# Recurrent attention with a feed-forward gate on eight cores: the key-value product moved ahead of the numerators, the output's last steps on GpSimd, and other places for the weight staging

## What is computed

```python
xn = layernorm(x)                                  # x: (8, 2048, 1024)
# recurrent (linear) attention, 16 heads of 64
q, k, v = (proj(xn, W) for W in (Wq, Wk, Wv))
qf, kf = softplus(q) + 1e-6, softplus(k) + 1e-6
kv = kv + outer(kf_t, v_t);  z = z + kf_t          # over t
out_t = (qf_t @ kv) / (qf_t . z + 1e-6)
s = out @ Wo.T
# feed-forward of the same xn, weights stored as integers with scales
h = layernorm(xn) * ln_gamma + ln_beta
y = silu(h @ dequant(fc1_q, fc1_scales) + fc1_bias)       # 4096 wide
zf = y @ dequant(fc2_q, fc2_scales) + fc2_bias
g = silu(xn + 0.5 * zf)
return x + s * g
```

## Time and profile before

| | us |
|---|---|
| median of the two runs | 4193.93 |
| the two runs | 4014.75 and 4373.1 |
| profiled execution, slowest core | 4024.7 |
| its span, first to last instruction | 4023.1 |
| TensorE matmul busy | 2843.4 (71% of the span) |
| VectorE busy | 1074.5 (27%) |
| ScalarE busy | 412.3 (10%) |
| GpSimd busy | 52.2 (1%) |

### The profile page before, as it was taken

The page is one execution under the profiler, slowest core; times in us unless marked ns, Lnnn a source line. Parts: engine busy times, 40 slices in busy tenths (PEclk is TensorE's granted clock), DMA queues, the critical chain, the costliest instruction groups (busy, mean ns, idle before and its releaser), DMA issues.

```text
span 4023.1 us, 40962 instructions; the slowest of 8 cores (4001.3 to 4023.1 us)
## 1 busy us (share of the span) xinstructions
PE 2843.4 (71%) x17088; PEld 2004.2 (50%) x17088; DVE 1074.5 (27%) x1533; ACT 412.3 (10%) x785; POOL 52.2 (1%) x103
## 2 busy tenths in 40 slices
PE   4678888757788777873087777777705668866668
PEld 3556665545566555652055555555403445544445
DVE  6332222131111211214612222222163221222221
ACT  0212222100000000000011111111100111111111
POOL 0000000000000000000100000000010000000000
PEclk9988888855665566565598888888857889888889
DMA  5111111122201122024600000000162110011110
GB/s 164 42 43 43 53 45 51 59 57 42 42 18 30 37 42 42 6 42 151 198 1 22 22 22 22 22 22 22 53 233 91 42 43 24 19 42 42 43 42 11
DMA packets 91414, 205.72 MB, mean 51 GB/s; under 512 B 37344, under 2 KB 53984, under 8 KB 85088
## 3 DMA queue, kind: packets, MB, share of 16 engines
q1 hardware_dynamic: 72368, 117.63, 9.8%
q0 software_dynamic: 14256, 68.69, 5.2%
q10 hardware_dynamic: 4608, 16.78, 1.4%
HBM read 152.75 MB, written 50.33 MB: 50 GB/s over the span
## 4 chain that ended last, share of the span: by engine, by line
PE 66%; DVE 15%; DMA 12%; issue 3%; DVEq 2%; ACT 1%; SPq 1%; POOL 0%; ACTq 0%; POOLq 0%
PE PS L142 17%; PE PS L143 17%; PE PS L144 17%; DVE AR L165 9%; DMA AR<-s 4%; PE PS L856 3%; PE PS L824 3%; DMA AR<-x_in 3%; DMA WA<-v_sc 2%; PE PS L847 2%; PE PS L850 2%; DVEq L166 2%; DVE WA L165 2%; DVE stats L165 1%; PE PS L829 1%
## 5 line engine op out<-in xcount | busy, mean ns | idle before, releaser
L142 PE MATMUL PS<-AR,WA 128*128 128x256 bf16 x3072 | 859.8, 280 | 44.0 <-DVE AR L567 29.2
L143 PE MATMUL PS<-AR,WA 128*128 128x256 bf16 x3072 | 859.6, 280 | 0.0
L144 PE MATMUL PS<-AR,WA 128*128 128x256 bf16 x3072 | 858.6, 279 | 0.0
L142 PE MATMUL PS<-WA,AR 128*128 128x512 bf16 x1536 | 597.6, 389 | 36.3 <-DVE AR L511 35.9
L143 PE MATMUL PS<-WA,AR 128*128 128x512 bf16 x1536 | 597.1, 389 | 0.0
L144 PE MATMUL PS<-WA,AR 128*128 128x512 bf16 x1536 | 595.5, 388 | 0.0
L912 PE MATMUL PS<-ident_s,AR 128*128 128x128 f32 x256 | 65.8, 426 | 686.6 <-DVEq L556 668.5
L571 DVE TENSOR_TENSOR AR<-YTMP,AR 128x256 bf16<-128x256 f32 x256 | 109.0, 426 | 1210.1 <-ACT AR L690 1210.1
L912 PEld LDWEIGHTS PS<-ident_s,AR 128*128 128x128 f32 x256 | 48.0, 220 | 705.5 <-issue 705.5
L142 PEld LDWEIGHTS PS<-AR,WA 128*128 128x128 bf16 x3072 | 308.3, 100 | 119.3 <-issue 52.9
L143 PEld LDWEIGHTS PS<-AR,WA 128*128 128x128 bf16 x3072 | 308.0, 100 | 66.3
(11 more groups left out here) (75 smaller groups left out, 2293.5 us busy)
## 6 DMA issues: line engine op xcount, KB each, us to landing
AR<-x_in SPq DMA_DIRECT2D x24, 1024.0 KB, 7.2
AR<-fc1q POOLq DMA_DIRECT2D x16, 1024.0 KB, 7.1
AR<-s POOLq DMA_DIRECT2D x16, 1024.0 KB, 9.1
AR<-fc2q POOLq DMA_DIRECT2D x32, 512.0 KB, 4.5
AR<-s POOLq DMA_DIRECT2D x32, 512.0 KB, 5.3
qf_sc<-AR SPq DMA_DIRECT2D x8, 1024.0 KB, 4.0
kf_sc<-AR SPq DMA_DIRECT2D x8, 1024.0 KB, 4.0
v_sc<-AR SPq DMA_DIRECT2D x8, 1024.0 KB, 6.5
```

The costliest lines, as they stand in the source:

```text
L142: tensor.matmul(out, lh, rh, start=start, stop=False)
L143: tensor.matmul(out, lh, rl, start=False, stop=False)
L144: return tensor.matmul(out, ll, rh, start=False, stop=stop)
```

## The change

Five things are changed together.

- **dKV moves.** TensorE does the 32 dKV matmuls after the A products and ahead of the numerators, with a count of its own (a2_dkv). kvs gets two buffers: numerators read kvsb[c % 2] while VectorE writes the new sum to kvsb[(c+1) % 2]. VectorE adds after the 16 masks.
- **The output's end.** In half 1 VectorE does one pass from PSUM (0.5 times it, plus stored z), in F_ZP. GpSimd adds xn, waits for Silu, multiplies by s and adds x. b2 is halved once and z of half 0 is stored halved. TensorE waits for VectorE's pass (f_t1) and no longer for the finished output. The output is stored from F_ZP, so the z load now waits for that store.
- **LayerNorm.** Gamma and beta are applied to both tiles of a chunk in one pass each.
- **Staging.** F_DEQ, F_SREP and the temporary lie elsewhere, so that F_X is free: SyncE loads x of the first chunk at the start of a half. The s load of half 1 waits for the dequantisation instead.
- **Waits on weights.** TensorE waits for 8 tiles before the first y step and for one more before each z step, instead of for all 24.

The diff, cut to its core:

```diff
-A2_KVS = 12320
+A2_KVS = [12320, 13632]
-F_DEQ = [0, 2048]
-F_SREP = [4096, 6144]
+F_DEQ = [8192, 10240]
+F_SREP = [12288, 14336]
@@ sync
                 for c in range(NC1):
-                    if c == 0:
-                        sync.wait_ge(f_deq[fi], 24)
-                    else:
+                    if c >= 1:
                         sync.wait_ge(f_xc[fi], c)
                     sync.dma_start(
                         out=ar(F_X, 2048).rearrange("p (s d) -> p s d", s=2),
...
                     if fi == 1:
+                        if c == 0:
+                            sync.wait_ge(f_deq[1], 24)
                         if c >= 1:
                             sync.wait_ge(f_zev[1], 2 * c)
...
+                        if c >= 1:
+                            sync.wait_ge(f_st[1], 16 * c)
                         sync.dma_start(
                             out=ar(F_ZP, 2048).rearrange("p (s d) -> p s d", s=2),
...
-                            in_=ar(F_OUT, 2048).rearrange("p (s d) -> p s d", s=2)
+                            in_=ar(F_ZP, 2048).rearrange("p (s d) -> p s d", s=2)
                         ).then_inc(f_st[1], 16)
@@ gpsimd
+                if fi == 1:
+                    for c in range(NC1):
+                        for s_ in range(2):
+                            gpsimd.wait_ge(f_t1, 2 * c + s_ + 1)
+                            og = ar(F_ZP + s_ * 1024, 1024)
+                            gpsimd.tensor_add(og, og, ar(F_XN + s_ * 1024, 1024))
+                            gpsimd.drain()
+                            gpsimd.engine_nop().then_inc(f_gv, 1)
+                            gpsimd.wait_ge(f_gs, 2 * c + s_ + 1)
+                            gpsimd.tensor_mul(og, og, ar(F_S + s_ * 1024, 1024))
+                            gpsimd.drain()
+                            gpsimd.tensor_add(og, og, ar(F_X + s_ * 1024, 1024))
+                            gpsimd.drain()
+                            gpsimd.engine_nop().then_inc(f_zev[1], 1)
+                            if s_ == 1:
+                                gpsimd.engine_nop().then_inc(f_xc[1], 1)
@@ vector
+                vector.wait_ge(a2_dkv, c + 1)
+                ksrc, kdst = kvsb[c % 2], kvsb[(c + 1) % 2]
+                vector.tensor_add(kdst[:, 0:455], ksrc[:, 0:455], PS[0:64, 0:455])
+                vector.tensor_add(kdst[:, 455:910], ksrc[:, 455:910], PS[0:64, 512:967])
+                vd.tensor_add(kdst[:, 910:1040], ksrc[:, 910:1040], PS[0:64, 3584:3714])
+                vector.engine_nop().then_inc(a2_kvu, 1)
                 for ts_ in range(2):
-                    vector.wait_ge(a2_nmm, 3 * c + ts_ + 1)
+                    vector.wait_ge(a2_nmm, 2 * c + ts_ + 1)
...
-                vector.wait_ge(a2_nmm, 3 * c + 3)
-                vector.tensor_add(kvs[:, 0:455], kvs[:, 0:455], PS[0:64, 0:455])
...
+                if fi == 0:
+                    vd.tensor_scalar_mul(b2rep[:], b2rep[:], 0.5)
...
-                    tmp = ar(8192, n)
+                    tmp = ar(F_XN, n)
...
-                        vd.tensor_mul(t_, t_, grep[:])
-                        vd.tensor_add(t_, t_, brep[:])
+                    gb = ar(F_LN2, 2048).rearrange("r (s d) -> r s d", d=1024)
+                    vd.tensor_tensor(gb, gb,
+                                     grep[:].unsqueeze(1).broadcast_to([P, 2, D]),
+                                     ALU.mult)
+                    vd.tensor_tensor(gb, gb,
+                                     brep[:].unsqueeze(1).broadcast_to([P, 2, D]),
+                                     ALU.add)
...
-                            vd.tensor_add(
+                            og = ar(F_ZP + s_ * 1024, 1024)
+                            vd.scalar_tensor_tensor(
                                 og,
                                 PS[:, (4 + 2 * s_) * 512:(4 + 2 * s_) * 512 + 1024],
-                                ar(F_ZP + s_ * 1024, 1024))
-                            vd.scalar_tensor_tensor(
-                                og, og, 0.5, ar(F_XN + s_ * 1024, 1024),
-                                ALU.mult, ALU.add).then_inc(f_gv, 1)
-                            vector.wait_ge(f_gs, 2 * c + s_ + 1)
-                            vd.tensor_mul(og, og, ar(F_S + s_ * 1024, 1024))
-                            vd.tensor_add(og, og, ar(F_X + s_ * 1024, 1024)
-                                          ).then_inc(f_zev[1], 1)
-                            if s_ == 1:
-                                vector.engine_nop().then_inc(f_xc[1], 1)
+                                0.5, og, ALU.mult, ALU.add).then_inc(f_t1, 1)
@@ tensor
                 if c >= 1:
-                    tensor.wait_ge(a2_kvu, c)
                     tensor.wait_ge(a2_sev, 2 * c)
...
                     inst.then_inc(a2_amm, 1)
+                tensor.wait_ge(a2_ktre, 4 * c + 4)
+                if c >= 1:
+                    tensor.wait_ge(a2_kvu, c)
+                if c == 0:
+                    tensor.wait_ge(a2_wev, 16)
+                for h in range(16):
+                    col = dkv_col(h)
+                    for sub in range(2):
+                        inst = tensor.matmul(
+                            PS[0:64, col:col + 65],
...
+                            start=(sub == 0), stop=(sub == 1))
+                        if h == 15 and sub == 1:
+                            inst.then_inc(a2_dkv, 1)
                 for ts_ in range(2):
...
-                                                 kvs[:, h * 65:h * 65 + 65],
+                                                 kvsb[c % 2][:, h * 65:h * 65 + 65],
...
-                tensor.wait_ge(f_deq[fi], 24)
...
                     if c >= 1:
-                        tensor.wait_ge(f_zev[fi], 2 * c)
+                        if fi == 1:
+                            tensor.wait_ge(f_t1, 2 * c)
+                        else:
+                            tensor.wait_ge(f_zev[fi], 2 * c)
...
+                            if c == 0 and ft == 0:
+                                tensor.wait_ge(f_deq[fi], 8)
...
+                            if c == 0:
+                                tensor.wait_ge(f_deq[fi], 9 + zt)
```

More of the change, by code:

```diff
@@ L129, in build_nc @@
         PS = es.enter_context(nc.psum_tensor("PS", [P, 4096], F32))
-        kvs = AR[0:64, A2_KVS:A2_KVS + 1040]
+        kvsb = [AR[0:64, A2_KVS[i]:A2_KVS[i] + 1040] for i in range(2)]
         WB = WA[:].bitcast(BF16)
@@ L222, in build_nc @@
         f_gv = sem("f_gv")
+        f_gg = sem("f_gg")
+        f_t1 = sem("f_t1")
+        a2_dkv = sem("a2_dkv")
         f_gs = sem("f_gs")
@@ L458, in _ @@
             if MP >= 2:
-                vd.memset(kvs[:], 0.0)
+                vd.memset(kvsb[0][:], 0.0)
             for sl in range(2 if MP >= 2 else 0):
@@ L514, in _ @@
                                              ALU.subtract).then_inc(a2_ntre, 1)
-                vector.wait_ge(a2_nmm, 3 * c + 3)
-                vector.tensor_add(kvs[:, 0:455], kvs[:, 0:455], PS[0:64, 0:455])
-                vector.tensor_add(kvs[:, 455:910], kvs[:, 455:910], PS[0:64, 512:967])
-                vd.tensor_add(kvs[:, 910:1040], kvs[:, 910:1040], PS[0:64, 3584:3714])
-                vector.engine_nop().then_inc(a2_kvu, 1)
             vector.engine_nop().then_inc(phb[1], 1)
@@ L577, in _ @@
                             vector.wait_ge(f_zmm[0], 2 * c + s_ + 1)
-                            vector.tensor_add(
+                            vector.scalar_tensor_tensor(
                                 ar(F_ZP + s_ * 1024, 1024),
                                 PS[:, (4 + 2 * s_) * 512:(4 + 2 * s_) * 512 + 1024],
-                                b2rep[:]).then_inc(f_zev[0], 1)
+                                0.5, b2rep[:],
+                                ALU.mult, ALU.add).then_inc(f_zev[0], 1)
                     else:
@@ L697, in _ @@
                             scalar.wait_ge(f_gv, 2 * c + s_ + 1)
-                            scalar.activation(ar(F_OUT + s_ * 1024, 1024),
-                                              ar(F_OUT + s_ * 1024, 1024), AF.Silu
+                            scalar.activation(ar(F_ZP + s_ * 1024, 1024),
+                                              ar(F_ZP + s_ * 1024, 1024), AF.Silu
                                               ).then_inc(f_gs, 1)
@@ L834, in _ @@
                     inst.then_inc(a2_amm, 1)
+                tensor.wait_ge(a2_ktre, 4 * c + 4)
[8 more added lines that the diff above has]
+                            PS[0:64, col:col + 65],
+                            WA[:, A2_KFT + h * 128 + sub * 64:
+                               A2_KFT + h * 128 + sub * 64 + 64],
+                            WA[:, A2_VA[sl] + sub * 1040 + h * 65:
+                               A2_VA[sl] + sub * 1040 + h * 65 + 65],
+                            start=(sub == 0), stop=(sub == 1))
+                        if h == 15 and sub == 1:
+                            inst.then_inc(a2_dkv, 1)
                 for ts_ in range(2):
@@ L880, in _ @@
```

(14 more changed lines are left out.)

5 lines of the change are left out of this document (2 added, 3 removed).

## The result

The changed kernel takes 4062.6 us (median of 19 runs), the kernel before 4021.1 us (median of 18). The ratio is 1.0096, with a 95% interval of 1.0077 to 1.0114: 39 us slower, where I had forecast 84.5. (Both sets hold some executions of 4200 to 4400 us in which the granted clock of a die was lower; the ratio leaves those out.) The growth is well clear of its interval, though it is under the 2% of a plain comparison. The time lies in my range, but the growth is under half of what I forecast, and the total alone doesn't say which term was off.

A forecast was written before the change was run, and what follows sets the result against it. TensorE was taken to carry the compute stages, standing still where a transfer or VectorE is last. Terms 57 - 1 + 42 - 7 - 6.5 = +84.5 us on 4024.7 gave 4109 us, range 4055 to 4165.

The forecast's parts named there:

- Part 1, the path: Attention: the hole behind the projection stays, the next chunk's loads don't come forward, the kvs sums cost nothing.
- the sum had -1: End of the attention stage: dKV and its adds no longer follow the last projection, -1 us.
- Part 1, the price: dKV ahead of the numerators: 7.9 us at clock 0.50, less 0.8 of cover, 7.1 us a chunk over eight chunks.
- The term +57: Attention total for dKV's move ahead of the numerators: +57 us, bounds +25 and +104.
- Rival A: Attention: clock rises halfway through dKV and holds through the numerator; stage -21 instead of +56, kernel 4032 us; chance 0.12.
- the ten from which I had said the stage gains: Rival A's threshold in attention: the stage gains once ten of the numerator's 16 pairs run at the high clock.
- Part 2: Second FFN half, output tail on GpSimd at 2.29 us a pass: +5.25 us a tail, eight times, +42 us.
- Parts 3 and 4: LayerNorm's gamma and beta in one pass for both tiles, -7 us; x loaded under the dequantisation, -6.5 us.
- the 2 us that I had taken: Dequantisation: the early x load delays the first weight tile by 2 us in each half, taken between 0 and 3.7.

The follow-up runs named there:

- e6: Kernel before plus 32 added matmuls a chunk ahead of the numerators, dKV's columns and count but over 64 rows; 4072.6 us, attention +50.5 us.
- e7: e3 with each half's first x load issued after the 20th weight tile instead of at the half's start; profiled execution 4005.1 us against e3's 4003.6.
- e3: Changed kernel with the output's add, multiply and add back on VectorE, all else as changed; 4005.5 us, ratio 0.9963 to the kernel before.
- e10: e3 with attention loads issued one chunk ahead and the first half's next x load ahead of SyncE's wait for z; 3815.1 us, ratio 0.9485.
- e5: Kernel before with dKV's 32 matmuls (128 rows) repeated each chunk ahead of the numerators, the original kept; 4025.3 us, attention 997.3 against 997.2.
- e2: Kernel before with only the output's end moved to GpSimd; 4077.7 us, ratio 1.0139, second half +56.7 us.
- e4: Changed kernel with two small GpSimd operations at the program's start, behind its first three transfers; profiled execution 4062.5 us.
- e9: Changed kernel with one small GpSimd add right behind the second half's last weight load; run once, execution 4051.4 us, second half 8.0 us less.

## Why the prediction was wrong

**Part 1, the path: right.** The hole behind the projection stayed and grew (16.22 to 19.18 us), the loads did not come forward, the kvs sums and the waits hid. From the last projection's end to the first weight load it was 4.5 us instead of 6.0 (medians), -1.5 where the sum had -1.

**Part 1, the price: the step that failed.** It reads "It now stands in the stretch at 0.50; twice that is 7.9 us". The stretch was at 0.50 with the matmuls that then stood in it, and I carried its clock over to matmuls of another kind. I had also taken the numerators behind dKV as unchanged. dKV took 5.3 us a chunk (42.0 over eight), and the numerators 4.2 us a chunk less (33.4 over eight). The term +57 should have been about +2; that is 55 of the sum's 84.5 us. The doubling was a little off too: e6 has 7.1 us at 1.2 GHz, so even with the clock down the term would have been +50.5.

**Rival A had the mechanism, with a chance of 0.12.** The clock rose in dKV and held into the numerator, but for six of the first tile's 16 pairs in the chunk shown and at most eight elsewhere, under the ten from which I had said the stage gains. dKV and the first tile together cost 1.2 us a chunk more, and the second tile's numerators gave back about as much. My argument against it was the fault: "40 us of nearly gapless fp32 matmuls stood at 0.50". Those were matmuls over 64 rows, or over 64 and 128 in turn, and e6 shows that 64 rows leave the clock down where 128 raise it. What I could have read in the earlier trace rows is that dKV differs from both neighbours in form: 128 rows and narrow weights. The clock of a stretch with other forms was no evidence for it, and a chance of 0.12 was too small.

**Part 2: right in place, 14 us short in size.** A pass was 2.34 us against 2.29, and the gaps between operations were 0.14 to 0.52 us against 0.1, which makes +6.3 us a tail where I had 5.25: 50 us over the eight tails, 8 more than forecast. Another 8 us are the drain behind the first elementwise operation after the weight loads, for which no row of before could speak. Together that is 58 us; the stages show 56. (By the medians of the cores an ordinary tail is nearer +6.1; what is left is within the scatter of the stages.)

**Parts 3 and 4: right.** Gamma and beta in one pass gave -4 and -5 us (forecast -3.5 each), x under the dequantisation -8.5 (forecast -6.5). VectorE's wait for x after the dequantisation is gone, and its wait for the first weight tile grew:

```profile
1860.89 2.29 DVE L165 SCALAR_TENSOR_TENSOR AR<-AR 128x2048 f32<-128x2048 f32 x1 [12.19 <-DMA AR<-s]
...
2004.92 3.49 DVE L165 TENSOR_SCALAR AR<-AR,stats 128x1024 f32<-128x1024 f32 x4 [0.17 <-issue]
```

12.19 us against 10.14 in the earlier trace rows, and 10.8 against 8.8 as the median of the eight cores: the 2 us that I had taken. e7 shows, though, that the load costs about the same when it comes late (the first tile's wait is back at 7.9 us there, and the stage no shorter). So the early place that I named is not what costs.

**The sum with what was measured:** +2 - 1.5 + 56 - 9 - 8.5 = +39 us, against 39 measured (41 by the medians of all runs). The two errors, 55 too much and 14 too little, had opposite signs. That the total stayed in the range is luck.

## What to carry to other kernels

When work is moved to another place of TensorE's stream, price it by what the work itself does to the clock, not by the clock of its new neighbours: look which forms of matmul, and over how many rows, stand where the clock rises in the trace, and count what the work behind it gains. Work handed to another engine counts at its full serial length if the next stage waits for it, however idle that engine is; here VectorE was idle too while GpSimd did in 2.34 us what it does in 1.23. And of five edits made together, the largest gain lay in none: two places in an in-order queue where a load stood behind a wait for something else were worth 190 us (e3's 4005.5 to e10's 3815.1).

## What was unexpected of the hardware

- TensorE's clock rose under fp32 matmuls over 128 rows with 64-column weights (5.2 us for 64 records that take 3.95 at the high level and 7.1 at the low one). It stayed at 1.2 GHz under the same matmuls over 64 rows (7.2 us), under A products over 64 rows that filled 20.20 of 20.20 us, and under matmuls over 128 rows with 128-column weights that filled 7.00 of 7.00 us.
- 47 us of full-height matmuls could be added in e5 with attention at 997.3 us instead of 997.2, since those behind them ran faster.
- Behind GpSimd's first elementwise operation after a long run of its own transfers the drain took some 8 us longer than the operation (10.52 us against a median of 2.42 in after; e2 and e4 have the same wait). With a small operation right behind the transfers, it was its drain that ended 8.2 us late (e9).
- A GpSimd pass with two fp32 inputs of 128x1024 took 2.34 us, VectorE's 1.23.
